# TensorE: the product that spreads the root stands behind the third up projection

## The reference

```python
xn = _layernorm(x)
s = recurrent_branch(xn)                 # conv, gates, linear scan over 1024 tokens, 192 channels
for i in range(6):                       # the deep branch
    xn = attn_layer(shift_tokens(xn), Wqkv[i], ...) + xn     # 16 heads of 64, local windows of 32
    xn = ffn_layer(shift_tokens(xn), ...) + xn
x = x + s * silu(xn)
# ffn_layer:
xn = (x - mu) / jnp.sqrt(var + 1e-05) * g + bln
a, gate = jnp.split(xn @ W1 + b1, 2, -1)            # 341 columns each
return a * gelu(gate) @ W2 + b2
```

## Time and profile before

| | |
|---|---|
| median of three runs | 1634.78 us |
| the profiled execution | 1636.79 us |
| its span, first to last instruction | 1634.9 us |
| TensorE busy (PE) | 1595.2 us, 98% |
| weight loads of TensorE (PEld) | 1369.1 us, 84% |
| VectorE busy (DVE) | 1396.1 us, 85% |
| ScalarE busy (ACT) | 1338.8 us, 82% |
| GpSimd busy (POOL) | 1321.5 us, 81% |
| mean granted TensorE clock | 0.995 |

### The profile page before, as it was taken

How to read it: one execution, slowest core, us unless ns; L and a number is a source line. 1 busy time by engine, 2 the same in 40 slices (tenths; PEclk the granted TensorE clock), 3 DMA queues, 4 the chain that set the end, 5 groups by cost and what they waited for, 6 DMA issues and landing times.

```text
span 1634.9 us, 50862 instructions
## 1 busy us (share of the span) xinstructions
PE 1595.2 (98%) x19920; PEld 1369.1 (84%) x19920; DVE 1396.1 (85%) x2021; ACT 1338.8 (82%) x2516; POOL 1321.5 (81%) x1278
## 2 busy tenths in 40 slices
PE   5899999999999999999999999999999999999997
PEld 3778888888888888888888888888888888888886
DVE  7788888888888888888888888888888899999975
ACT  5768888788888878888888888888888888888874
POOL 8888899888889888889888889888888777767741
PEclk9999999999999999999999999999999999999999
DMA  4334233433323344232344324244332332222232
GB/s 136 106 116 140 70 98 88 118 109 98 107 74 95 97 122 117 77 108 73 95 111 129 99 73 111 70 121 109 110 95 76 85 98 77 78 73 70 64 89 58
DMA packets 184872, 156.89 MB, mean 96 GB/s; under 512 B 111551, under 2 KB 156093, under 8 KB 184637
## 3 DMA queue, kind: packets, MB, share of 16 engines
q1 hardware_dynamic: 184636, 153.64, 33.7%
HBM read 27.56 MB, written 1.05 MB: 17 GB/s over the span
## 4 chain that ended last, share of the span: by engine, by line
PE 87%; ACT 5%; DVE 2%; issue 2%; POOL 2%; DMA 1%; SPq 0%; ACTq 0%; POOLq 0%; DVEq 0%
PE ps_pv L802 12%; PE ps_s L778 10%; PE ps_pv L821 10%; PE ps_tr L739 9%; PE ps_qn L714 9%; PE ps_qn L715 7%; PE ps_qn L716 7%; PE ps_tr L726 5%; PE ps_pv L811 3%; PE ps_qn L901 2%; PE ps_s L761 2%; PE ps_qn L902 2%; PE ps_qn L903 2%; PE ps_pv L859 1%; PE ps_qn L888 1%
## 5 line engine op out<-in xcount | busy, mean ns | idle before, releaser
L2027 POOL TENSOR_TENSOR qk<-qk,t 128x1024 f32<-128x1024 f32 x192 | 455.8, 2376 | 82.2 <-DVE qk L1545 81.6
L1542 DVE TENSOR_TENSOR t<-ps_qn,tab 128x512 f32<-128x512 f32 x384 | 264.4, 689 | 122.8 <-ACT sq L1140 111.5
L2039 POOL TENSOR_TENSOR qkr<-qk,rinv 128x1024 f32<-128x1024 f32 x192 | 361.5, 1904 | 8.0 <-POOL rinv L2019 0.8
L714 PE MATMUL ps_qn<-w_hi,xs_hi 128*128 128x512 f32 x576 | 261.1, 453 | 10.7 <-DVE qk L1545 8.2
L1127 ACT ACTIVATE pbd<-ps_tr 64x512 f32<-64x512 f32 x384 | 226.0, 589 | 55.2 <-PE ps_tr L726 51.4
L1545 DVE TENSOR_TENSOR qk<-ps_qn,tab 128x512 f32<-128x512 f32 x384 | 261.0, 680 | 0.0
L1140 ACT ACTIVATE sq<-ps_qn 128x512 f32<-128x512 f32 x384 | 228.6, 595 | 33.1 <-PE ps_qn L716 28.4
L1173 ACT ACTIVATE qbd<-ps_tr 64x512 f32<-64x512 f32 x384 | 226.9, 591 | 33.5 <-PE ps_tr L739 28.0
L715 PE MATMUL ps_qn<-w_lo,xs_hi 128*128 128x512 f32 x576 | 230.2, 400 | 0.0
L716 PE MATMUL ps_qn<-w_hi,xs_lo 128*128 128x512 f32 x576 | 229.7, 399 | 0.0
L1555 DVE TENSOR_REDUCE ss<-sq 128x32 f32<-128x2048 f32 x96 | 216.6, 2256 | 0.0
(11 more groups left out here) (177 smaller groups left out, 3180.6 us busy)
## 6 DMA issues: line engine op xcount, KB each, us to landing
v_own<-v_new SPq DMA_DIRECT2D x96, 512.0 KB, 3.3
v_back<-v_new SPq DMA_DIRECT2D x96, 384.0 KB, 3.5
v_back<-v_own SPq DMA_DIRECT2D x94, 128.0 KB, 2.3
kT<-kT SPq DMA_DIRECT2D x84, 128.0 KB, 2.8
w_raw<-in_Wqkv SPq DMA_DIRECT2D x18, 512.0 KB, 5.1
rot<-in_rot SPq DMA_DIRECT2D x48, 128.0 KB, 2.7
fx<-xmid SPq DMA_DIRECT2D x96, 64.0 KB, 2.1
xsh<-x SPq DMA_DIRECT2D x190, 32.0 KB, 2.6
```

Of the source, the lines that this page charges most:

```text
L714: mm(ps_qn[bank][:, :], xs_hi[b][:, :], w_hi[:, part], start=True, stop=False)
L1542: v.tensor_tensor(t2[:, part].rearrange("p (h s d) -> p h s d", s=2, d=DH // 2), swapped, tab[:, 2 * k + 1:2 * k + 2, :].rearrange("p o (s ...
L2027: g.tensor_tensor(qk[b][:, part], qk[b][:, part], t2[:, part], ALU.add).then_inc(added[b], 1)
L2039: g.tensor_tensor(qkr[b][:, part].rearrange("p (h d) -> p h d", d=DH), qk[b][:, part].rearrange("p (h d) -> p h d", d=DH), rinv[b][:, k * ...
```

## The change

Two calls in TensorE's `half(i, b)`, in the branch for b = 1, trade places. The order of the banks in `qn_order` and `pv_order` stays as it is, and no other engine's code is touched.

```diff
@@ -1013,8 +1013,8 @@
                             ffn_up(i, 1)
                             transpose_queries(i, b)
                         qkv(i, b, (4, 5))
+                        ffn_up(i, 2)
                         ffn_broadcast(i)
-                        ffn_up(i, 2)
                     scores(i, b, 0)
                     scores(i, b, 1)
```

## The result

The changed kernel takes 1647.34 us, the median of four runs (1646.1 to 1648.35), against 1635.4 for the kernel before in its four runs. The medians are 11.9 us apart. The ratio is 1.0068, with a 95% interval of 1.0055 to 1.008, which is 11.1 us slower, 9 to 13. The forecast was 11.7 us.

What follows compares the result with a forecast made beforehand. TensorE's queue was taken to bound the kernel. Ordinary steps 13.0 us, less 1.8 given back, plus 0.5 for recurrent steps made 11.7; added to the median 1634.8, 1646.5 us, with an 8-in-10 range of 1641 to 1650.5.

Steps and rivals of the forecast that it cites:

- The place: Between chunk 5 and the scores, b = 1: the array stands 0.36 us for chunk 4's bank; 36 steps, 13.0 us.
- the time from the reader's end to the first stream: At up 2: its first matmul streams 0.16 us after VectorE's copy of chunk 4 ends.
- My lower bound of 0.25: At up 2: a loss of 0.25 us a step if only the matmul, not its weight load, were held.
- The recurrent steps: Steps 40 to 47: up 2 first streams at +0.13 us, 8 x 0.13 = 1.0 us, of which 0.5 is taken back.
- What is given back in the ordinary steps: Behind the scores: a later TensorE wait vanishes, 0.05 us in each of 36 steps, 1.8 us back.
- the wait for the bank of chunk 3: TensorE's 0.05 us stand one half later, expected to vanish because VectorE's queue keeps its times for a while.
- The weight load not held: Rival at up 2: only the matmul waits, the array starts at +0.25; 7.2 us slower, 1642.0; 10%.
- the fallen clock: Rival on TensorE: the clock falls back once in each of 44 steps, 53 us more, about 1700; 2%.
- More than the range: Rival: later scores also delay VectorE's maxima and GpSimd's scaling, which meet a wait for `probs_ready`; over 1650.5; 6%.
- The faster one: Rival: up 2 done 0.07 us sooner speeds ScalarE and removes bank waits in both halves; 4.4 us less, 1630.4; 3%.
- VectorE's chain as what takes the loss back: Rival: VectorE's copies and rotations set the step, so up 2's wait only moves; 0 to 3 us, 1636; 6%.
- TensorE's queue sets the step: Ordinary steps, 31.69 us: time added to TensorE's queue is paid in full unless a later wait there shrinks.

Runs made afterwards that it cites:

- e2: The changed kernel with VectorE copying only 256 of the 512 columns of chunk 4 in b = 1: 1637.6 us, against 1635.8 before.
- e4: The kernel before with the spreading product moved between chunk 4 and chunk 5, up 2 behind chunk 5: 1650.0 us, against 1635.8 before.
- e7: The changed order only in the 31 steps that neither end a layer nor are recurrent, the order before elsewhere: 1646.5 us, against 1635.7 before.
- e11: The kernel before with only half of the columns of chunk 5 copied by VectorE in b = 1: 1635.1 us, against 1635.5 before.
- e1: The spreading product left out of the loop, the same program from either order; VectorE's scaling reads the identity: 1635.4 us, against 1635.8 before.

## Why the prediction was right

- **The place** was right: the spreading product was cover for the copy of chunk 4, and in the changed order the array stands. The loss at the place was 0.33 us and not 0.36. The term that was off is the time from the reader's end to the first stream, 0.16 by rows 5. Here the second matmul starts at 596.54, the first therefore streams from 596.42, 0.13 behind the copy's end at 596.29; in e2 it is 0.13 too. The weight load in front of it is 0.15 long in place of 0.19, which is the size of the gap, but this was not tested by itself. My lower bound of 0.25 (the load not held) fell: the load started 0.06 behind the copy. As for the rule in "TensorE: Matmul & The Clock Gate" of the Trainium skill, section "Step-by-step: what each phase is for", on weight loads pulled ahead, no pull over a semaphore shows here.
- **Nothing else in the change costs**: e2 with its late spreading product is 1.6 us over before, and its array still stands 0.05 a step for the bank.
- **The recurrent steps**: 0.13 predicted at the place, 0.10 measured. The prediction then took half of their 1.0 us off again, for engines that wait for one another. No such thing shows: the whole 0.10 reaches the next scores in each of the last seven, 0.8 us for the eight steps against the 0.5 in the sum.
- **What is given back in the ordinary steps**: the sum was close, 1.8 us predicted and 1.6 measured (5 layer ends of 0.33), but the place was wrong, so that this term agrees by luck. I had it at the wait for the bank of chunk 3, on the ground that VectorE's chain doesn't feel the delay. It does, by ScalarE. Timeline of the changed kernel behind the scores of step 18:

```profile
600.42 1.20 ACT L1127 ACTIVATE pbd<-ps_tr 64x512 f32<-64x512 f32 x2 [0.33 <-PE ps_tr L726]
...
603.34 0.60 ACT L1140 ACTIVATE sq<-ps_qn 128x512 f32<-128x512 f32 x1
...
603.97 0.69 DVE L1542 TENSOR_TENSOR t<-ps_qn,tab 128x512 f32<-128x512 f32 x1 [0.22 <-ACT sq L1140]
...
605.31 0.19 PEld L714 LDWEIGHTS ps_qn<-w_hi,xs_hi 128*128 128x128 f32 x1 [0.21 <-DVE qk L1545]
```

  ScalarE waits for the transposes, squares chunk 1 later, and VectorE rotates it later, so the wait of the weight load is 0.21 as it was the earlier trace rows. What did give the delay back is the end of a layer. There, in the kernel before, TensorE waits for the probabilities behind ScalarE's split of the weights, an event that the delay doesn't reach:

```profile
503.44 0.23 PEld L802 LDWEIGHTS ps_pv<-pbd,v_back 128*64 128x64 f32 x4 [0.66 <-issue]
503.47 0.34 PE L802 MATMUL ps_pv<-pbd,v_back 128*64 128x64 f32 x4 [0.26 <-ACT pbd L1127]
```

  In the changed kernel the same load has 0.37 idle before it and TensorE's matmul none, and it starts at 505.04: of the 1.89 by which the scores of step 15 were late, 1.57 are left.
- **The sum.** 31 steps of 0.315 (their mean without step 17), 5 steps with their loss given back, 8 of 0.11 make 9.8 + 0.9 = 10.7 us. The trace has 11.45. Step 17 adds 1.10 in place of 0.31:

```profile
563.58 1.29 DVE L1566 COPY v_new<-ps_qn 128x512 f32<-128x512 f32 x2 [1.40 <-DMA v_own<-v_new]
...
564.33 0.15 PEld L901 LDWEIGHTS ps_qn<-fxn_hi,w_hi 128*85 128x85 f32 x1 [1.29 <-DVE v_new L1566]
```

  The copy waits for a late transfer of the old values, and up 2 waits for the copy. With these 0.8 us the parts make 11.5, the measured sum within rounding. The forecast of 11.7 is so near it partly by luck: without the late transfer, which no term of it foresaw, the trace would have 10.7. VectorE's copies meet a late transfer in four of the thirteen traces (this one, e4, e7 and e11), in either order. In e7, step 17, the wait is 1.03, 0.42 longer than usual, and the step grows by 0.41 more than its neighbours. In the order of before such a delay falls on the cover first, as e11 shows in step 14:

```profile
463.52 1.02 DVE L1567 COPY v_new<-ps_qn 128x512 f32<-128x512 f32 x2 [1.09 <-DMA v_own<-v_new]
```

  The wait is 0.47 longer than the usual 0.62, and the step grows by 0.34.
- **The rivals.** The weight load not held and the fallen clock are out (the granted clock was 0.994 in the profiled run, against 0.995). More than the range is out by the time. The faster one hung on a bank that is free when chunk 5 ends; e2 has this, with the copy done 0.08 before, and it isn't faster. VectorE's chain as what takes the loss back is out for this change, since chunk 5 keeps its time. But the step at which I set it aside, "TensorE's queue sets the step", is half wrong: in the ordinary steps VectorE's chain is as long as TensorE's way. It didn't bend the forecast, because the change lengthens TensorE's way alone, and the longer of two equal ways sets the step. A forecast of a gain from the same reading would have failed, as that for e1 did.

## What to carry to other kernels

A short product of another chain that stands between the last use of a buffer and its next use is cover for the buffer's reader. Before it is moved, take the reader's end from the timeline and ask what the array does until then; without the cover it stands idle for that long, in each step. A small wait of an engine that is 98% busy (here 0.05 us for a bank) can be the mark of a second chain that is just as long. In the ordinary steps here, work added to either chain was paid nearly in full (0.31 of 0.33, 0.42 of 0.43), while work removed from one gained nothing until the other was shortened too.

## What the runs showed that was not expected

Leaving out 90 matmuls of 0.21 us each, some 19 us of TensorE's time, changed the kernel's time by -0.03% (-0.12 to +0.06%), though the recurrent steps among them did gain. The matmuls after a wait started to stream 0.13 us behind the reader's end with 85 columns of weights, and 0.16 with 128.
